# Gating the position and type loads of a graph-attention pass on the landing of gathered rows

## The reference, cut to what matters

```python
q, k, v = heads(nq @ Wq + bq), heads(nq @ Wk + bk), heads(x @ Wv + bv)
scores = sum(q[dst] * (k[src] + rel_bias[edge_type]), -1) / 4
seg_max = maximum(segment_max(scores, dst), 0)
exp_s = exp(scores - seg_max[dst])
attn = exp_s / (segment_sum(exp_s, dst)[dst] + 1e-8)
out = segment_sum(attn * v[src], dst) @ Wo + bo
```

## Time and profile before

| | |
|---|---|
| device time, median of 3 runs | 7942.78 us (7936.55 to 7952.53) |
| the profiled execution's own time | 7937.73 us |
| its span | 7936.0 us |
| PE, weight loads, DVE, ACT, Pool busy | 36%, 30%, 58%, 19%, 46% |
| mean granted clock of PE | 0.693 of full speed |
| blocks of the first edge pass | 1160.6 to 2830 us of the span |

### The profile page before, as it was taken

One profiled execution on the slowest core, in us unless ns is written; L12 is line 12 of the kernel. 1 busy time (PEld: TensorE's weight loads), 2 busy tenths in 40 slices (PEclk: granted clock), 3 DMA queues, 4 the chain that ended last, 5 costly groups with the idle time before them and its releaser, 6 DMA issues. The chain is left out here.

```text
span 7936.0 us, 112987 instructions
## 1 busy us (share of the span) xinstructions
PE 2893.9 (36%) x28649; PEld 2358.6 (30%) x28650; DVE 4600.8 (58%) x10704; ACT 1481.2 (19%) x3863; POOL 3660.9 (46%) x4402
## 2 busy tenths in 40 slices
PE   4179633455655532344233431345200000001334
PEld 3168512344545422334223431334200000000122
DVE  9677435566666636677467865677444444443333
ACT  0123100111111121222212222344311111110000
POOL 0155223333332324565445544554466666654555
PEclk9999996666777766676666766667555555555677
DMA  0034223334343523345333443334332222222334
GB/s 21 10 90 107 63 80 95 95 103 104 94 97 86 99 63 70 76 88 76 72 75 80 82 77 68 75 75 79 48 51 51 52 52 53 51 49 61 73 84 81
DMA packets 293996, 576.70 MB, mean 73 GB/s; under 512 B 137262, under 2 KB 182043, under 8 KB 273827
## 3 DMA queue, kind: packets, MB, share of 16 engines
q0 software_dynamic: 113232, 255.82, 21.2%
q1 hardware_dynamic: 142642, 278.18, 11.4%
q10 hardware_dynamic: 38049, 41.86, 1.7%
HBM read 479.10 MB, written 29.32 MB: 64 GB/s over the span
## 5 line engine op out<-in xcount | busy, mean ns | idle before, releaser
L3053 PE MATMUL bank<-tab,oh 128*128 128x136 bf16 x11700 | 894.3, 249 | 654.6 <-PEq L3045 387.2
L3053 PEld LDWEIGHTS bank<-tab,oh 128*128 128x128 bf16 x11700 | 865.0, 111 | 714.6 <-issue 714.5
L1422 PE MATMUL bank<-ident,hid 128*128 128x128 f32 x125 | 55.8, 447 | 2636.6 <-issue 1297.8
L1422 PEld LDWEIGHTS bank<-ident,hid 128*128 128x128 f32 x125 | 22.7, 182 | 2683.4 <-issue 2683.4
L2791 POOL DMA_INDIRECT land_a<-table,idx_a x624 | 665.3, 1066 | 228.4 <-issue 166.4
L2810 POOL DMA_INDIRECT land_r<-table,idx_r x492 | 502.5, 1021 | 214.9 <-issue 149.4
L2901 DVE TENSOR_TENSOR prod<-prod 128x128 f32<-128x128 f32 (+4 forms) x621 | 536.5, 864 | 14.6
L2976 ACT ACTIVATE rows<-bank 128x408 f32<-128x408 f32 x936 | 397.8, 515 | 753.9 <-ACTq L2975 554.9
L2602 PE MATMUL bank<-tab_l,oh_l 128*128 128x128 bf16 x3846 | 404.7, 240 | 210.3 <-issue 103.5
L2887 DVE TENSOR_TENSOR prod<-rows,bank 128x5376 f32<-128x5376 f32 x75 | 431.6, 5755 | 51.5 <-DVEq L2886 39.5
L3312 PE MATMUL bank<-tab_l,oh_l 128*128 128x384 bf16 x1250 | 260.1, 378 | 445.6 <-PEq L3306 333.2
(11 more groups left out here) (512 smaller groups left out, 8558.2 us busy)
## 6 DMA issues: line engine op xcount, KB each, us to landing
loc<-el_loc SPq DMA_DIRECT2D x78, 1088.0 KB
loc_l<-el_loc SPq DMA_DIRECT2D x52, 1088.0 KB
typ_l<-el_typ SPq DMA_DIRECT2D x52, 672.0 KB
rows_r<-land_r SPq DMA_DIRECT2D x123, 272.0 KB
landings_l<-landings_l SPq DMA_DIRECT2D x41, 784.0 KB
attr<-in_edge_attr ACTq DMA_DIRECT2D x75, 343.8 KB
land_a<-table,idx_a POOLq DMA_INDIRECT x936
land_r<-table,idx_r POOLq DMA_INDIRECT x492
```

The lines of the kernel that those rows point to most:

```text
L3053: last = pe.matmul(got[g % full][:, (c - of[0]) * W1:(c - of[0] + 1) * W1], oh[:, o], tab[:, t, x], start=n == 0, stop=n == len(parts) - 1 ...
```

## The change

The load of positions and types of a run gets one more wait ahead of the waits for free buffers: the count of landed gathers has to have reached that of the same run. The very first load is left out of it.

```diff
-                    def load_loc(r):
+                    def load_loc(r, ahead=True):
+                        if ahead:
+                            sp.wait_ge(s("got_a_l0"), r * (16 * FIRST) + 16 * FIRST)
                         sp.wait_ge(s("loc_free"), 1)
                         sp.sem_inc(s("loc_free"), -1)
...
                     load_list(0)
-                    load_loc(0)
+                    load_loc(0, ahead=False)
```

## The result

The change made the kernel slower: 7972.2 us median of 10 runs (7958.7 to 7985.2) against 7937.6 of 10 runs of the kernel before on the same chip (7905.5 to 7954.1), ratio 1.0046 [1.0031, 1.0061]. The forecast was 7886. Of the profiled executions the spans are 7970.7 and 7936.0 us, 34.7 us apart.

What follows compares the result with a forecast made beforehand. The exchange between PE and DVE bounds the pass, with PE slowed by landing gathers. Gains of 30 us (fourteen blocks) and 27 us (nine) off 7937.73 give 7881, 7886 as median; eight-in-ten range 7825 to 7985.

Steps and rivals of the forecast that it cites:

- plain loads don't disturb PE here, landing gathers do, by five times: First edge pass: PE starts 18.5 matmuls a us beside loads, 5 in 10 us with only gathers in flight.
- the ahead keys done by 2363.5: One-turn block: sixth key product, last of the keys PE makes ahead, at about 2363.5 in place of 2371.18.
- the 84 matmuls under shelter: Two- and three-turn blocks: beside the moved load PE does 84 narrow-key matmuls at 10 to 11 a us by 1563.
- 2.1 us x 14 and 3 us x 9: Gains: 2.1 us in each of fourteen one-turn blocks (30 us), 3 us in each of nine others (27 us).
- from 2361 to 2371 PE worked at the ahead keys at 3.5 matmuls a us: One-turn block: 5.10 us wait plus 0.69 us product taken as the time of a group's 20 matmuls.
- The move of the load: Load goes out some 4 us after Pool's last gather for the next block; at 1553.2 in the two-turn block.
- not within 7 us: Sign of being right: in nearly all one-turn blocks the sixth key product comes within 7 us of the start.
- The turn gathers come 5 us later, and are used only at the end of the block.: Two- and three-turn blocks: the moved load delays the overflow turn's gathers by 5 us, taken to be used only at block end.
- One turn: Fourteen one-turn blocks: 55.2 us each in place of 57.3, with the load over 2362.5 to 2374.6; 30 us gained.
- The slower rival: PE stays slow until the last gather lands, later than before: 5 us in nine blocks, 2 in fourteen, 73 us, 8016; chance 0.25.
- The types come late: Two-turn blocks: a 16 us load instead of 13.2 makes DVE wait 1 to 3 us a block, 10 to 25 us; no own chance.
- Range: Whole kernel: forecast's own range 7815 to 7930; for eight in ten 7825 to 7985, the upper end reaching into slower outcomes.

Runs made afterwards that it cites:

- e8: Kernel before with each gathered row cut to 24 and 16 words after the first block, same number of gathers: 7984.0 us, ratio 1.0000.
- e9: Kernel before without the four relation gathers of each overflow turn, their rows stale: 7756.7 us, ratio 0.9779.
- e2b: Kernel before with the wait added only for the loads of one-turn blocks: 7957.3 us, ratio 1.0028.
- r_before: Kernel before, unchanged, timed again for its trace on that chip: 7933.1 us, ratio 0.9995.
- e10: Kernel before with nearly all loads of positions and types cut to one column (80 KB in place of 2.4 MB): 7994.2 us, ratio 1.0002.
- the halves of the first set: Kernel before with the wait only for loads issued in blocks with two or more turns (7436.2 us, 1.0105), or only in one-turn blocks (7424.0 us, 1.0088).
- r_after: The changed kernel as it is, beside the kernel before on another chip: 8012.3 us, ratio 1.0031.
- e12: The changed kernel as it is, repeated beside the kernel before: 8024.2 us, ratio 1.0038.

## Why the prediction was wrong

**The step that failed** is "plain loads don't disturb PE here, landing gathers do, by five times". The rows were right, 74 starts in 4 us and then 5 in 10, but two things changed between them, and I took the wrong one: the gathers' data began, and Pool was 3 us into issuing them (from 2347.82). e8 took nine tenths of the bytes away and nothing changed; e9 took a quarter of a block's gathers away and the blocks shrank by 4 us for 5 us of issuing. The load only seemed a shelter since in the earlier trace rows it was ending as the hold-up began; beside the moved load PE started 5 matmuls in 7 us. Everything costed from it (the ahead keys done by 2363.5, the 84 matmuls under shelter, 2.1 us x 14 and 3 us x 9) had no ground.

**A reading that was wrong** is that from 2361 to 2371 PE worked at the ahead keys at 3.5 matmuls a us. PE and ACT in the kernel before:

```profile
2361.63 0.37 PE L2575 MATMUL bank<-rel_l,oht_l 128*128 128x128 bf16 x2 [0.35 <-issue]
...
2371.72 0.82 PE L2641 MATMUL bank<-w_g,hid_t 128*128 128x144 f32 x2 [9.50 <-PEq L2640]
```

```profile
2371.18 0.28 ACT L2458 ACTIVATE hid_t<-bank 128x128 f32<-128x128 f32 x1 [18.26 <-ACTq L2478]
```

The last ahead key was taken up at about 2361.7, so no start was left for a load that goes out at 2362.5 to shelter. DVE and ACT got the results 9.4 us after that, of matmuls already taken up. A count of starts is not a rate of finished work.

**The move of the load** came as worked out: 2338.21, 4.1 us after Pool's last gather of the next run at 2334.12 in a one-turn block, and +8.4 us in the two-turn block (forecast 1553.2, +9.2). In that one-turn block, start 2333.80, the sixth key product comes at 2348.03, +14.2, and not within 7 us.

**"The turn gathers come 5 us later, and are used only at the end of the block."** The first half holds: 5.2 us. The second is the step by which the nine blocks lost: turn two can't be issued before turn one is copied, so Pool's issuing moved by 6.5 us in the block shown and stood beside all of DVE's value products instead of the first part of them. What was late next was a value product, and I had looked at the comparison of types. The term measured +2.4 us a block where I had taken -3.

**One turn.** I had -2.1 us a block; it was +2.15. On one chip e2b beside r_before shows that it is the loss of the load ahead of the gathers that costs it: 59.6 us a block in place of 57.5. The forecast had given the load's place ahead a worth of half a us (2350.5 in place of 2351). By what means it shortens blocks is open. e10 and e8 don't bear it out in time: they are within 4 and 6 us of before on their chips, where before was not traced.

**The slower rival** had the sign, and its condition (under 5 starts a us beside both) was met: 0.7. But it priced the delay of the keys' end to the last *landing*, and in the nine blocks the key wait grew by 3.7 us only. Its 73 us were 35.

**The types come late** cost nothing on the chip of the result (0.26 us before their comparison, since PE's hold-up puts that at +28) and nearly everything where before takes 7360: an estimate of 76 + 64 = 140 us from the halves of the first set; the whole change was not timed there. My bound of 16 us for the load was a bound on its length, and I did not ask what would happen to the cover if DVE came to it earlier.

**Range.** 7972 lies in it for the slower rival's sake. Against the rule that I had set aside ("Trainium Architecture — The Big Picture" of the Trainium skill, What this means for kernel authors: engine side and DMA side of SBUF can't contend), my "the trace does not agree" was hasty: 35 starts in 4 us at DMA share 0.94 agree with it, and so does e8.

What stays open: what in Pool's issuing holds PE's results up, why not from the first gather on, and why on some chips alone; why the load ahead shortens some one-turn blocks; and whether the kernel before has such blocks on the chips near 7990, where no trace of it was taken. There r_after's and e12's loss of 23 to 34 us is covered by the nine blocks alone (25 us), which would mean that it has none.

No version tried beats the kernel before and keeps its output. e9's 178 us say where to look: fewer indirect gathers issued by Pool, for instance one row that holds table and relation values. That was not tried.

## What to carry to other kernels

When an engine stalls beside several things, list all that start and stop with the stall, the issuing engine's own work too, and find a window in which only one of them differs; here the trace of the kernel after had one, just behind Pool's last issue. Before reading a stretch without starts as a slow engine, see whether the engine had anything left to start, and who waits for its results. Moving a transfer later costs first what is chained behind the transfers it now shares with (turn one's rows, turn two's issue, the phase beside them), and then its cover, which is as long as the slowest thing ahead of its consumer and goes when that gets faster. A gain that rests on a pattern of one chip should be looked for on a second before it is built on.

## What the runs showed of the hardware that was not expected

- The same kernel took 7360 us in two sets and 7935 to 7990 in the others, by the chip, with 0.2% and 0.7% between the lowest and the highest run of a set. In the first pass the difference lies in PE's hold-up: 127 starts in 8.5 us with seven gathers being issued on one, 5 in 7 us with six on another. Of the 574 us between the traces of the kernel before on two chips, 337 are in blocks 0 to 23 of this pass; the rest was not looked into.
- The hold-up depends on the number of indirect gathers that Pool issues and hardly on their bytes: unchanged with a tenth of them, 4.0 us less for four gathers (5.0 us of issuing) less a one-turn block. In the blocks shown it ended 1.3 and 2.1 us after Pool's last issue; in two traces with the full load ahead it ended before it in 17 of 26 blocks.
- Results can be late by far more than their matmuls' starts: 14 us from the last start to the product, with the DMA engines at share 0.16.
